# Feed-forward stage of a four-layer kernel: layer norm's moments of samples 3 to 8 made by matmuls with a constant tile, root by ScalarE

## The chip, the core and the metric

The kernel runs on one core of a Trainium2 chip. The metric is device time in microseconds (us) of one execution. Five engines work from queues of their own, each in order: TensorE (PE; its weight loads, PEld, overlap its matmuls), VectorE (DVE), ScalarE (ACT), GpSimd (POOL) and SyncE (SP), which issues the DMAs. They wait for one another through semaphores written out by hand.

## What is computed

Eight samples of 512 tokens by 512 channels pass through a rotation, a conditioned residual block, a low-rank steering layer and a transformer block. The change lies in the last layer's feed-forward part:

```python
def layernorm(x, gamma, beta):
    mu = jnp.mean(x, axis=-1, keepdims=True)
    var = jnp.var(x, axis=-1, keepdims=True)
    return (x - mu) * jax.lax.rsqrt(var + EPS) * gamma + beta
x1 = x + attn_out
h2 = layernorm(x1, gamma2, beta2)
ff = jax.nn.gelu(h2 @ W1 + b1, approximate=False) @ W2 + b2
x2 = x1 + ff
return x + g * (x2 - x)
```

All is float32. Products keep that accuracy by splitting each operand into a high part, rounded to the matmul's type (`F32R`), and the low rest, and taking three matmuls: high by high, high by low, low by high.

## The kernel before

A sample `x` of the feed-forward stage lies in SBUF with its channels over the 128 partitions: `x[:, j, :]` for j = 0 to 3 holds 128 channels by 512 tokens. Layer norm takes its moments over the channels, so over the partitions and over j.

In the code samples are b = 0 to 7. Samples b = 0 and 1 have paths of their own. From b = 1 on the first layer's product with W1 is made in 2x2 blocks by seven products in place of eight: a pair of hidden tiles is made by `product(pair, k)`, k in the order 1, 6, 7, 4, 5, 2, 3, each six matmuls of 256 columns. VectorE adds them up in five steps, `partial_of(pair, 0)` to `partial_of(pair, 4)`; steps 3 and 4 leave the two finished hidden tiles, one after the other. ScalarE takes Gelu of each and rounds it (`pair_high(pair, True)`, then `pair_high(pair, False)`: k_act, k_act_hi), VectorE makes the low rest (`pair_low`: k_act_lo), and TensorE multiplies with W2 (`second_product`, twelve matmuls of 512 columns for each hidden tile, cut into halves "0, 1" and "2, 3").

One sample is eight such pairs, called periods p = 0 to 7 here. `period(b, p)` writes out the order of each engine; n is the pair whose second product is running, n + 1 the one that is made meanwhile. TensorE in a period: product 1, product 6, second product of the first hidden tile (0, 1), product 7, (2, 3), product 4, product 5, second product of the second tile (0, 1), product 2, product 3, (2, 3). VectorE: `pair_low(n, False)`, `partial_of(n+1, 0)` and 1, then 2 and 3, `pair_low(n+1, True)`, `partial_of(n+1, 4)`. ScalarE: `pair_high(n, False)`, `copy_first(n+1)`, `pair_high(n+1, True)`. Products 4 and 5 write over the places in PSUM of products 1 and 6: product 4 waits until `partial_of(n+1, 0)` is done (L2237's first 256-column add of a pair). Product 1 waits for `partial_of(n, 3)`, product 7 for `partial_of(n, 4)`, product 2 for `partial_of(n+1, 1)`. The second product of a hidden tile waits for its `pair_low` (L2216).

Layer norm of the next sample is put between, in periods 2 to 5: `add_attention` (p = 2: x plus attention's result), `tokens` (TensorE turns x, sixteen 128x128 transposes, eight at the end of p = 2 and eight in p = 3, L2451), `statistics` (VectorE's mean and variance of each token from PSUM, two tiles at the start of p = 3 and two near its end, L2164 and L2166), the root by GpSimd (variance plus epsilon to the power -0.5, 128x4, L2100 and L2102), `spread` (p = 4: eight transposes that turn mean and root back and repeat them over the partitions, L2467 and L2471), `centre` (p = 4, after `partial_of(n+1, 3)`: x minus mean, four VectorE operations, L2177), `normalise` (p = 5, four more, L2183), ScalarE's `scale`, then the splitting into blocks.

`samples()` runs these periods for b = 2 to 7, which prepares samples b = 3 to 7 (five of them). The periods of b = 1 and before, which prepare b = 2, are written out one by one in `vector_tail`, `scalar_tail` and `tensor_tail`, mixed with the making of W1's factors for pairs 5 to 7 (`factor_high`, `factor_low`, `factor_sums`).

Of the kernel before, what the change touches and what calls it, by code (L numbers as in the profile page):

```python
# [18 lines left out]
P = 128  # L19
# [1906 lines left out]
def feed_forward_engines(nc, ctx, io, keep, psum, attention):  # L1926
# [29 lines left out]
    whole_tile = keep["stack_f"][1][:, 7, :]  # L1956
    partial = rows_of(keep["raw"][:, 2:4, :, :])[:, 6:8, :].rearrange("p n (h s) -> p (n h) s", h=2)
# [16 lines left out]
    added, summed, biased, gated = sem("added"), sem("summed"), sem("biased"), sem("gated")  # L1974
    given_ld, factor_sum, factor_hi, factor_lo = sem("given_ld"), sem("factor_sum"), sem("factor_hi"), sem("factor_lo")
# [30 lines left out]
    made_of = lambda part: given[part[1]][:, :, part[2], :].rearrange("p k a c -> p a k c")  # L2006

# [85 lines left out]
    def gpsimd(pool):  # L2093
        for b in range(B):
# [3 lines left out]
            if b + 1 < B:  # L2098
                pool.wait_ge(mv_set, T * (b + 1))
                pool.tensor_scalar(var[:], mv[:, :, 1], LN_EPS, None, ALU.add).then_inc(var_set, 1)  # L2100
                pool.wait_ge(var_set, b + 1)
                pool.tensor_tensor(rstd[:], var[:], keep["minus_half"][:], ALU.pow).then_inc(rstd_set, 1)  # L2102

    def vector(dve):
# [54 lines left out]
        def statistics(b, t):  # L2159
            if b == 1:  # L2160
                dve.wait_ge(tok_set, t + 1)
            else:
                dve.wait_ge(tin_full, T * (b - 1) + t + 1)
            dve.bn_stats(st[:, t, :], tok[:, t, :] if b == 1 else turn(t)).then_inc(stat_set, 1)  # L2164
            dve.wait_ge(stat_set, T * (b - 1) + t + 1)
            dve.bn_aggr(mv[:, t, :], st[:, t, :]).then_inc(mv_set, 1)  # L2166

# [6 lines left out]
        def centre(b):  # L2174
            dve.wait_ge(tback_full, J + 2 * (b - 2) + 1)
            for j in range(J):
                dve.tensor_tensor(tok[:, j, :], x[:, j, :], turn(0), ALU.subtract).then_inc(normed, 1)  # L2177

        def normalise(b):
            dve.wait_ge(tback_full, J + 2 * (b - 1))  # L2180
            for j in range(J):
                dve.wait_ge(normed, T + 2 * J * (b - 2) + j + 1)
                dve.tensor_tensor(tok[:, j, :], tok[:, j, :], turn(1), ALU.mult).then_inc(normed, 1)  # L2183
# [63 lines left out]
        def period(b, p):  # L2247
# [7 lines left out]
            if more and p == 3:  # L2255
                statistics(b + 1, 0)
                statistics(b + 1, 1)
# [15 lines left out]
            if more and p == 2:  # L2273
                add_attention(b + 1)
            if more and p == 5:
# [8 lines left out]
            if more and p == 3:  # L2284
                statistics(b + 1, 2)
                statistics(b + 1, 3)
# [21 lines left out]
        return steps(w1_low, w2_low, factor_low, factor_sums, add_attention, start_result, statistics, normalise_first, block_low, block_sums,  # L2308
                     split, finish, pair_low, partial_of, centre, normalise, samples)

    def scalar(act):
# [29 lines left out]
        def tokens(t):  # L2341
# [3 lines left out]
            act.activation(tok[:, t, :], turn(t), ACT.Copy).then_inc(tok_set, 1)  # L2345

# [56 lines left out]
        def period(b, p):  # L2403
# [4 lines left out]
            if n + 1 < HALF * (B - 1):  # L2408
                copy_first(n + 1)
            if n in EARLY_PARTS:  # L2410
# [22 lines left out]
        return steps(w1_high, w2_high, factor_high, tokens, scale, block_high, gelu, copy_first, pair_high, samples)  # L2433

    def tensor(pe):
        def tokens(b, t):
            if t == 0:
                pe.wait_ge(mid_set, J * b)
                if b == 1:
                    attention["results_taken"](pe)  # L2440
                elif b == 2:
                    pe.wait_ge(h_set, J)
                else:
                    pe.wait_ge(normed, T + 2 * J * (b - 2))
            if t >= 2:
                if b == 1:
                    pe.wait_ge(tok_set, t - 1)
                else:
                    pe.wait_ge(stat_set, T * (b - 1) + t - 1)
# [13 lines left out]
        def spread(b):  # L2463

            pe.wait_ge(mv_set, T * b)
            for t in range(T):
                last = pe.transpose(turn(0)[:, t * P:(t + 1) * P], mv[:, t, 0:1].to_broadcast([P, P]), ident[:])  # L2467
            last.then_inc(tback_full, 1)
            pe.wait_ge(rstd_set, b)
            for t in range(T):  # L2470
                last = pe.transpose(turn(1)[:, t * P:(t + 1) * P], rstd[:, t:t + 1].to_broadcast([P, P]), ident[:])  # L2471
            last.then_inc(tback_full, 1)
# [57 lines left out]
        def period(b, p):  # L2530
# [8 lines left out]
            second_product(at, m[0], 0, 1)  # L2539
            if first:  # L2540
# [15 lines left out]
            if more and p == 2:  # L2556
                tokens(b + 1, 0)
                tokens(b + 1, 1)
# [6 lines left out]
        return steps(tokens, back, spread, first_product, second_product, product, samples)  # L2565
# [570 lines left out]
def vector_tail(att, ff):  # L3136
# [83 lines left out]
    ff.statistics(1, 0)  # L3220
# [7 lines left out]
    for k in range(1, 4):  # L3228
        ff.statistics(1, k)
# [80 lines left out]
    ff.partial_of(3, 3)  # L3310
    ff.factor_low(6, 0)
    ff.pair_low(3, True)
    ff.partial_of(3, 4)
    ff.statistics(2, 0)
    ff.statistics(2, 1)
# [4 lines left out]
    ff.statistics(2, 2)  # L3320
# [3 lines left out]
    ff.statistics(2, 3)  # L3324
# [8 lines left out]
    ff.factor_low(7, 0)  # L3333
    ff.normalise(2)
    ff.partial_of(5, 4)
# [279 lines left out]
def scalar_tail(att, ff):  # L3615
# [164 lines left out]
    ff.pair_high(2, False)  # L3780
    ff.factor_high(6, 0)
# [782 lines left out]
```

## Time and profile before

| | |
|---|---|
| median of 3 runs | 1610.72 us (1610.68 to 1611.48) |
| span of the profiled execution | 1610.9 us |
| TensorE busy in it | 1585.8 us (98%) |
| VectorE, ScalarE, GpSimd busy | 1166.6, 982.8, 410.9 us |
| mean granted TensorE clock | 0.995 |
| feed-forward periods of samples | from about 1010 us to the end, one sample in about 86.5 us |

How to read it: times of the views count from the span's start. A matmul's own time holds the way through the array; the distance from one start to the next says what it takes of TensorE when the queue is full. The chain of waits gives such distances. VectorE's operations overlap by about 0.08 us where one does not need the other's result.

### The profile page before, as it was taken

To read this page: it belongs to the slowest core of one execution; us is meant where nothing else is said; L and a number is where in the kernel's file an instruction comes from. 1 tells how busy PE (TensorE), PEld (TensorE's weight loads), DVE (VectorE), ACT (ScalarE), POOL (GpSimd) and SP (SyncE) were. 2 spreads that over 40 slices of the span, in tenths; PEclk is the share of its full clock that TensorE was granted. 3 is DMA by queue.
4 is the path that set the end of the run, shared out by engine and by line. 5 is a ranking of instruction groups with operands and counts; after the bars stand their busy time and mean duration, and the time that the engine had idled before them with its cause. 6 is when DMAs were issued, how large, how long until landed. Compare 5 with 4: busy or idle time off the path is not lost.

```text
span 1610.9 us, 27177 instructions
## 1 busy us (share of the span) xinstructions
PE 1585.8 (98%) x9296; PEld 1299.5 (81%) x9298; DVE 1166.6 (72%) x2767; ACT 982.8 (61%) x2331; POOL 410.9 (26%) x605
## 2 busy tenths in 40 slices
PE   7999999999999999999999999999999999999999
PEld 4688786777777777777777688898999999999998
DVE  7999888786969686868778576785655656565643
ACT  6888766887878787878778755352433324242422
POOL 8998810313222313131312110201010110202010
PEclk8999999999999999999999999999999999999999
DMA  7042135543545444444337435866464555556361
GB/s 308 0 183 97 66 126 126 149 130 92 138 95 139 100 115 122 111 116 115 88 90 214 167 152 207 303 262 232 178 234 170 213 225 188 212 178 265 142 211 68
DMA packets 62257, 254.79 MB, mean 158 GB/s; under 512 B 10628, under 2 KB 16004, under 8 KB 46760
## 3 DMA queue, kind: packets, MB, share of 16 engines
q1 hardware_dynamic: 62120, 253.06, 48.2%
q8 instruction: 74, 1.21, 0.3%
q14 instruction: 63, 0.52, 0.1%
HBM read 153.93 MB, written 48.23 MB: 125 GB/s over the span
## 4 chain that ended last, share of the span: by engine, by line
PE 90%; POOL 3%; DMA 2%; DVE 2%; ACT 1%; issue 1%; SPq 1%; POOLq 0%; DVEq 0%; ACTq 0%
PE psum L83 24%; PE psum L84 23%; PE psum L85 23%; PE psum L1529 5%; PE psum L1549 5%; PE psum L1579 4%; PE psum L1470 1%; DMA k_weights<-w_factors 1%; PE psum L1478 1%; PE psum L2451 1%; DMA k_raw<-in_t_w 1%; POOL k_gs_square L252 1%; POOL k_gs_root L247 1%; ACT psum L1229 1%; POOL k_gs_scaled L256 1%
## 5 line engine op out<-in xcount | busy, mean ns | idle before, releaser
L1229 ACT ACTIVATE psum<-psum,b_mx 128x512 f32<-128x512 f32 (+3 forms) x512 | 258.9, 509 | 63.2 <-DVE b_mx L990 62.0
L990 DVE CUSTOM_DVE_ANT_0 psum<-psum,b_mask 128x512 f32<-128x512 f32 (+3 forms) x512 | 244.7, 506 | 53.0 <-PE psum L1529 48.1
L2398 ACT ACTIVATE k_act<-k_stack_f,k_smalls 128x512 f32<-128x512 f32 x112 | 80.9, 722 | 303.6 <-DVE k_stack_f L2237 297.1
L1241 ACT ACTIVATE k_exps<-psum 128x512 f32<-128x512 f32 (+1 forms) x384 | 194.6, 532 | 59.4 <-PE psum L1549 58.1
L864 POOL TENSOR_SCALAR_AFFINE_SELECT k_exps<-k_exps 128x256 f32<-128x256 f32 x256 | 96.4, 413 | 381.0 <-ACT k_exps L1241 379.1
L2097 POOL TENSOR_SCALAR k_result<-k_result,k_pb 128x512 f32<-128x512 f32 x32 | 59.2, 1866 | 434.9 <-DVE k_result L2156 434.9
L2216 DVE TENSOR_TENSOR k_act_lo<-k_act,k_act_hi 128x512 fp32r<-128x512 f32 x112 | 77.2, 690 | 120.6 <-ACT k_act_hi L2401 120.6
L83 PE MATMUL psum<-k_act_hi,k_w_hi 128*128 128x512 f32 x384 | 150.8, 393 | 0.0
L84 PE MATMUL psum<-k_act_lo,k_w_hi 128*128 128x512 f32 x384 | 150.5, 392 | 0.0
L85 PE MATMUL psum<-k_act_hi,k_w_lo 128*128 128x512 f32 x384 | 150.2, 391 | 0.0
L2237 DVE TENSOR_TENSOR k_raw<-psum,k_raw 128x256 f32<-128x256 f32 x168 | 70.5, 421 | 106.0 <-PE psum L85 95.4
L1529 PE MATMUL psum<-k_stack 96*128 96x512 f32 (+3 forms) x512 | 142.6, 330 | 3.1 <-DMA k_stack<-k_samples 2.0
L85 PE MATMUL psum<-k_normed,k_weights 128*128 128x512 f32 (+1 forms) x384 | 144.3, 376 | 0.0
L1549 PE MATMUL psum<-k_stack 98*128 98x512 f32 (+3 forms) x512 | 134.8, 332 | 0.6 <-ACT k_exps L1241 0.3
L83 PE MATMUL psum<-k_normed,k_weights 128*128 128x512 f32 (+1 forms) x320 | 126.0, 394 | 0.0
L84 PE MATMUL psum<-k_normed,k_weights 128*128 128x512 f32 (+1 forms) x320 | 120.0, 375 | 0.0
L1529 PEld LDWEIGHTS psum<-k_stack 96*128 96x128 f32 x512 | 93.6, 190 | 29.9 <-issue 8.8
L1549 PEld LDWEIGHTS psum<-k_stack 98*128 98x128 f32 x512 | 91.0, 189 | 27.7 <-issue 9.6
L1229 ACT ACTIVATION_READ_ACCUMULATOR psum<-psum,b_mx 128x1 f32 x512 | 108.6, 212 | 0.0
L85 PEld LDWEIGHTS psum<-k_act_hi,k_w_lo 128*128 128x128 f32 x384 | 72.1, 188 | 16.2
L85 PEld LDWEIGHTS psum<-k_normed,k_weights 128*128 128x128 f32 x384 | 73.0, 190 | 14.1
L83 PE MATMUL psum<-k_h,k_stack 128*128 128x256 f32 x294 | 82.6, 281 | 0.0
(372 smaller groups left out, 4418.2 us busy)
## 6 DMA issues: line engine op xcount, KB each, us to landing
k_stack<-w_factors SPq DMA_DIRECT2D x35, 1792.0 KB, 7.7
k_stack<-k_samples SPq DMA_DIRECT2D x384, 128.0 KB, 2.4
k_weights<-w_factors SPq DMA_DIRECT2D x17, 1792.0 KB, 7.5
x<-k_tokens SPq DMA_DIRECT2D x10, 1024.0 KB, 4.3
k_tokens<-x SPq DMA_DIRECT2D x8, 1024.0 KB, 5.1
d<-k_result SPq DMA_DIRECT2D x32, 256.0 KB, 2.9
k_raw<-x SPq DMA_DIRECT2D x8, 1024.0 KB, 4.8
k_raw<-d SPq DMA_DIRECT2D x8, 1024.0 KB, 7.1
```

Source lines behind the costliest of these rows:

```text
L83: pe.matmul(out, w_hi, x_hi, start=start and k == 0, stop=False)
L84: pe.matmul(out, w_hi, x_lo, start=False, stop=False)
L85: last = pe.matmul(out, w_lo, x_hi, start=False, stop=stop and k == n - 1)
L864: pool.affine_select(out=own, in_=own, compare_op=ALU.is_ge, fill=0.0, base=0, pattern=[[0, 2], [1, P]], channel_multiplier=-1).then_inc(c ...
L990: last = dve.tensor_tensor_reduce(got, got, mask[:, S - width:S], -INV_SQRT_DH, -2.0 * MASKED, ALU.add, ALU.min, mx[n % 2][:, h, t:t + 1])
L1229: act.activation(sc(n, u)[:, at:at + width], sc(n, u)[:, at:at + width], ACT.Exp, bias=mx[n % 2][:, h, t:t + 1], scale=-1.0, accum_out=sum ...
L1241: act.activation(exps[n % 2][:, h, at:at + width], by_key(n, u)[:, 0:width], ACT.Exp, scale=INV_SQRT_DH).then_inc(k_act, 1)
L1529: last = pe.matmul(sc(n, u)[:, at:at + width], stack[n % 2][0:3 * DH, 2 * h, t * P:(t + 1) * P], stack[n % 2][0:3 * DH, 2 * h + 1, 0:width ...
L1549: last = pe.matmul(by_key(n, u)[:, at:at + width], stack[n % 2][0:3 * DH + 2, 2 * h + 1, j * P:(j + 1) * P], stack[n % 2][0:3 * DH + 2, 2 ...
L2216: dve.tensor_tensor(act_lo[n % 2], act_f[:], act_hi[n % 2].bitcast(F32), ALU.subtract).then_inc(act_lo_set, 1)
L2237: dve.tensor_tensor(out, got, other, ALU.add).then_inc(partial_set, 1)
L2398: act.activation(act_f[:], whole_tile, ACT.Gelu, bias=small(smalls, "b1", 2 * pair % M + second)).then_inc(pair_gelu, 1)
```

## The change

For samples b = 2 to 7 layer norm's moments no longer pass through turned tokens. The sums over j are made by VectorE, the sum over the partitions by a matmul with a tile that holds 1/512 everywhere (`mean_of`), which leaves the mean repeated in every partition. ScalarE squares x, VectorE adds the squares, a second pair of matmuls gives the mean square. Root: ScalarE's Ln and Exp (-0.5 times) from one table set, named in the code, then one step of refinement by VectorE. The mean (x's sum) and the squares' sum are split in high and low, two matmuls of 512 columns each. Moved: `tokens`, `statistics` and `spread` are gone for these samples; `token_sum` stands in p = 2 after `partial_of(n+1, 3)`, `square_sum` at the start of p = 3, `variance` in p = 4 between `partial_of(n+1, 0)` and 1, `refine` in p = 4 ahead of `partial_of(n+1, 2)`. GpSimd has no part of it any more.

```diff
+        def token_sum(b):
+            dve.wait_ge(mid_set, J * (b - 1) + 2)
+            dve.tensor_tensor(sum_f, x[:, 0, :], x[:, 1, :], ALU.add).then_inc(sums_set, 1)
+            for j in (2, 3):
+                dve.wait_ge(mid_set, J * (b - 1) + j + 1)
+                wait_sums(dve, b, j - 1)
+                dve.tensor_tensor(sum_f, sum_f, x[:, j, :], ALU.add).then_inc(sums_set, 1)
+            wait_sums(dve, b, 3)
+            dve.tensor_copy(sum_hi, sum_f).then_inc(sums_set, 1)
+            wait_sums(dve, b, 4)
+            dve.tensor_tensor(sum_lo, sum_f, sum_hi.bitcast(F32), ALU.subtract).then_inc(sums_set, 1)
+        def square_sum(b):
...
+        def variance(b):
+            dve.wait_ge(tback_full, J + 2 * (b - 2) + 2)
+            wait_squares(dve, b, J)
+            dve.tensor_tensor(var_f, turn(1), sum_f, ALU.subtract).then_inc(stat_set, 1)
+            wait_statistics(dve, b, 1)
+            dve.tensor_scalar(var_f, var_f, 0.0, LN_EPS, ALU.max, ALU.add).then_inc(stat_set, 1)
+        def refine(b):
+            wait_rough(dve, b, 2)
+            dve.tensor_tensor(var_f, var_f, sum_f, ALU.mult).then_inc(stat_set, 1)
+            wait_statistics(dve, b, 3)
+            dve.scalar_tensor_tensor(var_f, var_f, -0.5, sum_f, ALU.mult, ALU.mult).then_inc(stat_set, 1)
+            wait_statistics(dve, b, 4)
+            dve.scalar_tensor_tensor(sum_f, var_f, 1.5, sum_f, ALU.add, ALU.mult).then_inc(stat_set, 1)
@@ vector, period
             if more and p == 3:
-                statistics(b + 1, 0)
-                statistics(b + 1, 1)
+                square_sum(b + 1)
...
+                if more and p == 4:
+                    variance(b + 1)
                 partial_of(n + 1, 1)
...
+            if more and p == 4:
+                refine(b + 1)
...
-            if more and p == 3:
-                statistics(b + 1, 2)
-                statistics(b + 1, 3)
+            if more and p == 2:
+                token_sum(b + 1)
             if more and p == 4:
                 centre(b + 1)
@@ scalar
+        def squares(b):
+            for j in range(J):
+                act.wait_ge(mid_set, J * (b - 1) + j + 1)
+                act.activation(tok[:, j, :], x[:, j, :], ACT.Square).then_inc(tok_set, 1)
+        def rough_rstd(b):
+            act.preload_act_table_set("natural_log_exp_and_others")
+            wait_statistics(act, b, 2)
+            act.activation(sum_f, var_f, ACT.Ln).then_inc(rstd_set, 1)
+            wait_rough(act, b, 1)
+            act.activation(sum_f, sum_f, ACT.Exp, scale=-0.5).then_inc(rstd_set, 1)
+            act.preload_act_table_set("gelu_and_others")
@@ tensor
+        def mean_product(b):
...
+            wait_sums(pe, b, 5)
+            pe.matmul(turn(0), mean_of[:], sum_hi, start=True, stop=False)
+            pe.matmul(turn(0), mean_of[:], sum_lo, start=False, stop=True).then_inc(tback_full, 1)
+        def square_product(b):
+            wait_sums(pe, b, 10)
+            pe.matmul(turn(1), mean_of[:], squares_r[:, 1, :], start=True, stop=False)
+            pe.matmul(turn(1), mean_of[:], squares_r[:, 2, :], start=False, stop=True).then_inc(tback_full, 1)
@@ tensor, period
+            if more and p == 4:
+                square_product(b + 1)
             if first:
                 product(n, 7)
             second_product(at, m[0], 2, 3)
             if more and p == 3:
-                tokens(b + 1, 2)
-                tokens(b + 1, 3)
-            if more and p == 4:
-                spread(b + 1)
+                mean_product(b + 1)
...
-            if more and p == 2:
-                tokens(b + 1, 0)
-                tokens(b + 1, 1)
```

`square_sum` has the five operations of `token_sum`, on the squares and in place. ScalarE's `squares` stand in p = 2 and one more `mean_square` (the mean's square, from PSUM) in p = 3, both between `copy_first` and `pair_high(n+1, True)`; `rough_rstd` is there in p = 4. The lists written out for b = 2 get the same steps: `token_sum(2)` after `partial_of(3, 3)`, `square_sum(2)` ahead of `partial_of(4, 0)`, `variance(2)` ahead of `pair_low(4, True)`, `refine(2)` after `factor_low(7, 0)`, and `partial_of(5, 4)` ahead of `normalise(2)` instead of behind it.

## Rows read from the trace of the kernel before

**Rows 1.** Page, part 1: busy time, share of the span and instructions of each engine.
```profile
PE 1585.8 (98%) x9296; PEld 1299.5 (81%) x9298; DVE 1166.6 (72%) x2767; ACT 982.8 (61%) x2331; POOL 410.9 (26%) x605
```
**Rows 2.** Busy time by stretch: PE, PEld, DVE, ACT, POOL, then clock, DMA.
```profile
1280.00:1370.00 90.00, 90.00 (x573) 81.31 (x572) 53.82 (x98) 32.11 (x53) 8.91 (x6) 1.00 0.58 214
```
**Rows 3.** Chain of waits, one sample: start, time it takes, what.
```profile
1300.19 0.23 PE psum L85
1300.43 0.87 PE psum L2451 x8
```
**Rows 4.** Timeline of PE, periods 3 to 5 of one sample: start, duration, operation.
```profile
1302.57 0.39 PE L83 MATMUL psum<-k_act_hi,k_w_hi 128*128 128x512 f32 x1
...
1306.83 0.36 PE L83 MATMUL psum<-k_weights 128*128 128x256 f32 x1
...
1315.37 0.28 PE L83 MATMUL psum<-k_normed,k_stack 128*128 128x256 f32 x1
...
1325.40 0.39 PE L83 MATMUL psum<-k_act_hi,k_w_hi 128*128 128x512 f32 x1
```
**Rows 5.** Timeline of DVE, periods 2 to 6 of the same sample; brackets: idle time before.
```profile
1297.03 0.68 DVE L2237 TENSOR_TENSOR k_stack_f<-psum,k_raw 128x512 f32<-128x512 f32 x1
1299.30 0.69 DVE L2216 TENSOR_TENSOR k_act_lo<-k_act,k_act_hi 128x512 fp32r<-128x512 f32 x1 [1.58 <-ACT k_act_hi L2401]
...
1302.17 0.69 DVE L2216 TENSOR_TENSOR k_act_lo<-k_act,k_act_hi 128x512 fp32r<-128x512 f32 x1 [1.59 <-ACT k_act_hi L2401]
...
1304.41 0.95 DVE L2237 TENSOR_TENSOR k_raw<-psum,k_raw 128x256 f32<-128x256 f32 x2
...
1319.95 0.42 DVE L2237 TENSOR_TENSOR k_raw<-psum,k_raw 128x256 f32<-128x256 f32 x1 [3.17 <-PE psum L85]
...
1323.27 0.68 DVE L2216 TENSOR_TENSOR k_act_lo<-k_act,k_act_hi 128x512 fp32r<-128x512 f32 x1
...
1339.36 0.69 DVE L2197 TENSOR_TENSOR k_tokens<-k_tokens 128x512 f32<-128x512 f32 x1
1340.09 0.69 DVE L2199 TENSOR_TENSOR k_tokens<-k_tokens 128x512 f32<-128x512 f32 x1
```
**Rows 6.** Single lines of the code: count, duration in ns (shortest/median/longest), first and last start.
```profile
L907 DVE CAST b_steer<-k_row_f x1: 424/424/424, 40.7 to 40.7; 2x512 fp32r<-2x512 f32 x1
L2171 DVE TENSOR_SCALAR k_tokens<-k_tokens,b_mv,b_rstd x4: 544/546/549, 952.0 to 953.4; 128x512 f32<-128x512 f32 x4
L2156 DVE SCALAR_TENSOR_TENSOR k_result<-k_raw,k_pb x32: 742/747/1100, 924.3 to 1545.2; 128x512 f32<-128x512 f32 x32
L2371 ACT ACTIVATE k_h<-k_tokens x28: 613/616/636, 974.3 to 1514.7; 128x512 fp32r<-128x512 f32 x28
L2380 ACT ACT_TABLE_LOAD  x1: 1283/1283/1283, 905.8 to 905.8; - x1
```
**Rows 7.** Timeline of DVE, the written-out part that prepares sample b = 2.
```profile
1042.47 0.69 DVE L2164 BATCH_NORM_STATS2 b_st<-psum 128x6 f32<-128x512 f32 x1
...
1044.09 0.40 DVE L2237 TENSOR_TENSOR k_raw<-psum,k_raw 128x256 f32<-128x256 f32 x1
...
1063.30 0.42 DVE L2237 TENSOR_TENSOR k_raw<-psum,k_raw 128x256 f32<-128x256 f32 x1 [0.37 <-ACT k_raw L2391]
```
**Rows 8.** Timeline of PE and ACT in the same part.
```profile
1044.55 0.39 PE L83 MATMUL psum<-k_h,k_weights 128*128 128x256 f32 x1
1064.70 0.28 PE L83 MATMUL psum<-k_h,k_stack 128*128 128x256 f32 x1
1039.46 0.42 ACT L2335 ACTIVATE k_stack<-b_mask 128x256 fp32r<-128x256 f32 x1 [7.43 <-DMA k_early<-in_w]
```
**Rows 9.** Early stage: PE's longest wait, and the two stretches from there (columns as in 2).
```profile
10.33 1.87 PE L541 MATMUL psum<-k_sines,k_raw 128*128 128x8 f32 x8 [3.69 <-DMA k_raw<-in_t_w]
...
10.00:20.00 10.00, 7.22 (x25) 3.49 (x27) 8.38 (x21) 9.13 (x15) 8.60 (x10) 0.50 1.01 422
20.00:30.00 10.00, 9.77 (x68) 6.01 (x69) 7.92 (x16) 6.33 (x10) 8.41 (x11) 0.99 1.02 421
```

More of the change, by code:

```diff
@@ new lines, in square_sum @@
+        def square_sum(b):
+            wait_squares(dve, b, 1)
+            dve.tensor_tensor(tok[:, 0, :], tok[:, 0, :], tok[:, 1, :], ALU.add).then_inc(sums_set, 1)
+            for j in (2, 3):
+                wait_squares(dve, b, j)
+                wait_sums(dve, b, 4 + j)
+                dve.tensor_tensor(tok[:, 0, :], tok[:, 0, :], tok[:, j, :], ALU.add).then_inc(sums_set, 1)
+            wait_sums(dve, b, 8)
+            dve.tensor_copy(squares_r[:, 1, :], tok[:, 0, :]).then_inc(sums_set, 1)
+            wait_sums(dve, b, 9)
+            dve.tensor_tensor(squares_r[:, 2, :], tok[:, 0, :], squares_r[:, 1, :].bitcast(F32), ALU.subtract).then_inc(sums_set, 1)
@@ L2306, in samples @@
                 finish(B - 1, j)
-        return steps(w1_low, w2_low, factor_low, factor_sums, add_attention, start_result, statistics, normalise_first, block_low, block_sums,
+        return steps(w1_low, w2_low, factor_low, factor_sums, add_attention, start_result, statistics, token_sum, square_sum, variance, refine, normalise_first, block_low, block_sums,
                      split, finish, pair_low, partial_of, centre, normalise, samples)
@@ L2409, in period @@
                 copy_first(n + 1)
+            if more and p == 2:
+                squares(b + 1)
+            if more and p == 3:
+                mean_square(b + 1)
+            if more and p == 4:
+                rough_rstd(b + 1)
             if n in EARLY_PARTS:
@@ L2539, in period @@
             second_product(at, m[0], 0, 1)
+            if more and p == 4:
+                square_product(b + 1)
             if first:
@@ L2563, in samples @@
                     period(b, p)
-        return steps(tokens, back, spread, first_product, second_product, product, samples)
+        return steps(tokens, back, mean_product, square_product, first_product, second_product, product, samples)
     return {"sync": sync, "gpsimd": gpsimd, "vector": vector, "scalar": scalar, "tensor": tensor}
@@ L3219, in vector_tail @@
     ff.w1_low(4)
-    ff.statistics(1, 0)
+    ff.statistics(0)
     ff.split(4)
@@ L3228, in vector_tail @@
     for k in range(1, 4):
-        ff.statistics(1, k)
+        ff.statistics(k)
     ff.split(6)
@@ L3310, in vector_tail @@
     ff.partial_of(3, 3)
+    ff.token_sum(2)
     ff.factor_low(6, 0)
@@ L3313, in vector_tail @@
     ff.partial_of(3, 4)
-    ff.statistics(2, 0)
-    ff.statistics(2, 1)
+    ff.square_sum(2)
     ff.partial_of(4, 0)
@@ L3323, in vector_tail @@
         ff.partial_of(4, k)
-    ff.statistics(2, 3)
+    ff.variance(2)
     ff.pair_low(4, True)
@@ L3333, in vector_tail @@
     ff.factor_low(7, 0)
+    ff.refine(2)
+    ff.partial_of(5, 4)
     ff.normalise(2)
-    ff.partial_of(5, 4)
     ff.factor_low(7, 1)
@@ L3780, in scalar_tail @@
     ff.pair_high(2, False)
+    ff.squares(2)
     ff.factor_high(6, 0)
@@ L3786, in scalar_tail @@
     ff.factor_high(6, 2)
+    ff.mean_square(2)
     ff.pair_high(4, True)
@@ L3790, in scalar_tail @@
     ff.pair_high(4, False)
+    ff.rough_rstd(2)
     ff.factor_high(7, 0)
     ff.factor_high(7, 1)
+    ff.pair_high(5, True)
     ff.scale(2, 0)
-    ff.pair_high(5, True)
     ff.scale(2, 1)
@@ L4383, in tensor_tail @@
     ff.second_product(22, 7, 2, 3)
-    ff.tokens(2, 2)
+    ff.mean_product(2)
     ff.product(4, 5)
```

89 lines of the change are left out of this document (44 added, 45 removed).

## Prediction

> **What bounds the kernel now.** I read the page's busy shares first: TensorE 98%, VectorE 72%, ScalarE 61% [rows 1]. Then busy time by stretch in the part that the change touches: of 90 us TensorE is busy 90.00, VectorE 53.82, ScalarE 32.11 [rows 2]. So here TensorE alone sets the end: a microsecond taken from its queue is a microsecond of the kernel, provided it never waits. Third, the chain of waits: it runs through TensorE's matmuls and through the transposes, which take 0.87 us for eight [rows 3]. Last the timelines of the engines through one sample [rows 4, 5], because the change gives work to an engine on which TensorE depends, and an average share does not say whether that work falls at a moment with room.
>
> **TensorE's side, which gains.** Removed for each of six samples: 24 transposes, three times 0.87, together 2.61 us. Added: four matmuls of 512 columns at 0.23 each [rows 3], 0.92 us. Net 1.69 us a sample, 10.1 us in all, if nothing waits. For the five samples of the loop, place by place: TensorE is 0.87 early from period 3 on, 0.87 - 0.46 more after `mean_product` in the middle of period 3, and 0.87 - 0.46 more after period 4.
>
> **VectorE's side: the sizes.** A chain of dependent 512-column adds starts every 0.73 us (1339.36, 1340.09 [rows 5]); so three adds 2.18. The copy that rounds: the only row of a cast from SBUF to fp32r of this length takes 0.42, on two partitions [rows 6]; I take it with 0.04 for the dependence, 0.46, and 0.73 as upper end, that of an add; below 0.42 there is no row of a 512-element operation. The subtraction holds the queue for 0.61 more (0.69 less the 0.08 of overlap). Sum of `token_sum`, and of `square_sum`: 3.25 us each, 3.52 by the upper end. The Trainium skill, page "VectorE: DVE Perf Modes", section "Mode 2×_2P — use both read ports for one tensor", says that an operation with one source, all in SBUF, makes two results in a cycle in fp32 too, and that one with two tensors cannot. By it the cast stays at the row's length on 128 partitions and the sums at 3.25; without it they would be 3.52 and each stall below 0.5 longer. No row here shows the cast on 128 partitions. `variance`: 0.73 and 0.55 [rows 6]. `refine`: 0.73 + 0.79 + 0.67 = 2.2, with 0.75 for the two three-operand steps [rows 6]. Removed: `statistics`, four times 0.8. VectorE has room for the sum in 86 us; what counts is the place.
>
> **Period 2, `token_sum`.** Before, `partial_of(n+1, 3)` starts at 1297.03 and VectorE then sits 1.58 us until `pair_low(n+1, True)` at 1299.30 [rows 5]. Now VectorE is free at 1297.03 + 0.60 = 1297.63, works until 1300.88, and `pair_low` starts there: 1.58 late, done at 1301.57. TensorE wants it at 1302.57 [rows 4] less 0.87 = 1301.70. It just fits; no stall, but the slack is used up. ScalarE's four squares (0.62 each, as its rounding copies [rows 6]) follow the adds of `add_attention` one by one and end before Gelu's input is there: nothing. The second hidden tile's chain (`partial_of(n+1, 4)`, Gelu, rounding) starts 1.58 later too, so `pair_low(n, False)` of period 3 starts at 1302.17 + 1.58 = 1303.75 [rows 5].
>
> **Period 3, `square_sum`: the step that decides.** It stands ahead of `partial_of(n+1, 0)`, and product 4 may not start before that is done. VectorE is through with `pair_low` at 1304.36, with the squares at 1307.61; `partial_of(n+1, 0)` ends at 1308.03, and with 0.1 for the signal (it took 0.06 from 1044.09 + 0.40 to 1044.55 [rows 7, 8]) product 4 can start at 1308.1. Before it was done by 1304.41 + 0.42 = 1304.83 [rows 5], two microseconds ahead of product 4 at 1306.83 [rows 4]. Now TensorE arrives there at 1306.83 - 0.87 - 0.87 + 0.46 = 1305.55. It stalls for 2.55 us and goes on 1.3 us later than before. Everything that VectorE and ScalarE do next hangs on products 5 to 3, so it moves by the same 1.3.
>
> **Period 4, `variance`, root, `refine`.** The square product stands after the second product's first half, before ended at 1315.37 [rows 4]: now 1315.37 + 1.3 + 0.46 = 1317.1. `variance` runs from 1317.3 to 1318.6. `partial_of(n+1, 0)` is already through and 1 is not urgent. Ln and Exp at 0.65 each (bounds 0.62 and the 0.72 of a Gelu with a bias) end at 1320.05. `refine` holds VectorE until 1322.25, where before `partial_of(n+1, 2)` came at 1319.95 [rows 5]: 2.3 us late, and with it `partial_of(n+1, 3)`, Gelu, `centre`. `pair_low(n+1, True)` starts at 1323.27 + 2.3 = 1325.57 and is there at 1326.36; TensorE, which is now 1.3 - 0.41 = 0.89 later than before, wants it at 1325.40 + 0.89 = 1326.29 [rows 4, 5]. Stall 0.1; up to 0.7 with the longer lengths. The two table loads (1.28 us each [rows 6]) cost nothing: the first lies ahead of Ln while ScalarE would wait for `variance` anyway, the second between Exp at 1320.05 and Gelu's input near 1323.3. If that cover were gone, each would add its 1.3 us to the same chain. `centre` and `normalise` keep their lengths; for periods 6 and 7 I take no stall and have no rows for it here; 0.4 us a sample go into the upper end.
>
> Sum for one sample of the loop: 2.55 + 0.1 - 1.69 = +0.96, near 1.0; five of them +5.0. GpSimd's two small operations go, and are priced at nothing: they lay beside TensorE's work.
>
> **The written-out part (b = 2).** `token_sum` fits: ScalarE and VectorE wait for a DMA until 1039.46 there, after 7.43 us of idle ScalarE [rows 8], and TensorE's first groups of transposes only shorten the way to that same date, so part of the 1.69 is not gained. `square_sum` takes the place of two statistics that held VectorE from 1042.47 to 1044.09 [rows 7]: 3.25 for 1.62, so `partial_of(4, 0)` and product 4, which restarted at 1044.55 right behind it [rows 8], are 1.65 late. Fewer transposes behind it (sixteen gone at 1.74, two pairs of matmuls come at 0.92) bring that to +0.8. Then `variance` (1.2) ahead of `pair_low(4, True)` and `refine` (2.2) ahead of `normalise(2)`, less the other two statistics, push `partial_of(6, 0)` from 1063.30 [rows 7] to about 1066.8; product 4 of pair 6 stood at 1064.70 [rows 8] + 0.8 = 1065.5 and can start at 1067.3: a stall of 1.8. Sum +2.6; the factors' DMA of pair 7, which moves with `factor_low(6, 3)` by 2 us, can add to it: 2 to 4, I take 2.7.
>
> **Forecast.** +5.0 + 2.7 = +7.7 us on the span of 1610.9, which is the median of the runs (1610.7) within 0.2: 1618.4 us, slower by 0.5%. Its own range: the loop's samples +0.6 (a stall shorter by 0.4) to +2.0 (the cast as long as an add makes 0.5 more in period 3, period 5 and the unworked periods add another 0.5 together), the written-out part 2 to 4: 1615.9 to 1624.9.
>
> **Rivals.** (a) The cover holds, the change gives what it takes from TensorE: 10.1 us, 1600.6. It needs `partial_of(n+1, 0)` of period 3 to be done 2.5 us sooner than I place it. For it: VectorE is idle 40% of the time [rows 2]. Against: queues are in order and product 4's wait is in the code. Chance 0.09. (b) Stall and saving cancel: the sums take 0.6 each in place of 0.73 for dependent adds, both sums 1 us shorter together, and period 3's stall is about 1.5: 1609 to 1613. Against: dependent adds of this length show 0.73 [rows 5]. Chance 0.08. (c) Slower by more, through the clock. After TensorE's wait of 3.69 us the stretch from 10 to 20 us shows 0.50, which is 1.2 GHz in place of 2.4, and 0.99 again in the stretch after [rows 9]. If a stall of 2.5 us did the same, each of the seven would cost up to half of ten microseconds: about +30, 1640 or more. Against: the wait in the early stage is half as long again, and the ones before us would each stand alone between stretches of full work. The Trainium skill, page "TensorE: Matmul & The Clock Gate", states such a gate with these two levels, and the trace agrees on the levels. Chance 0.04. (d) The change doesn't do what it says, that is, a step is late because the compiler adds table loads or the square is not in Gelu's set: one load more in period 2, 1.3 us more before Gelu there, and then `pair_low(n+1, True)` is late by up to 1.3 in period 3; the later stall takes that up in part: 1620 to 1625, inside the forecast's range. Chance 0.05, the forecast itself 0.74.
>
> **How the numbers follow.** Slower by over 0.2% (3.2 us; about what a measurement of this kernel can tell from no change) are the forecast, (c) and (d): 0.83. Same 0.08, faster 0.09. The range: the forecast's own with (d) holds 0.79 less what its bounds leave out; I reach down into (b), to 1612, and to 1625 at the top.
>
> **What would show it.** In the profile after: TensorE waits some 2.5 us for VectorE's 256-column add (L2237's line) once in each sample, at a product's first matmul; `token_sum` and `square_sum` of 3.2 us each on VectorE, the latter right ahead of that add; a stretch of 90 us with TensorE busy about 87; clock 1.00; table loads of 1.28 with no TensorE wait behind them. Wrong if TensorE's busy stretches stay at 90.00 of 90 (then a), if the stall in period 3 is about 1.5 (b), or if the clock falls (c); wrong in its second term if period 5 shows a stall of a microsecond.

## The result, and the profile after

| | before | after |
|---|---|---|
| median | 1610.7 us (4 runs, 1609.9 to 1611.5) | 1626.6 us (4 runs, 1625.6 to 1628.6) |
| span of the profiled execution | 1610.9 us | 1623.9 us |
| mean granted TensorE clock | 0.995 | 0.991 |
| ratio of the times | | 1.010 [1.009, 1.011] |

Slower by 1.0%, twice the 0.5% that was forecast, and 1.6 us above the end of the range. A second round of the changed kernel (below) gave 1626.2. The profiled spans differ by 13.0 us and the medians by 15.9, because the execution profiled after had reached the feed-forward samples early: its first result of sample b = 0 is written at 1005.2 us against 1008.3 before. In the profiled executions of all the kernels below that date lies between 1003.4 and 1008.3 us, though none of them changes that first part. So all that follows is counted from there on: before 602.64 us are left, after 618.67, that is +16.0.

The page's first line of the kernel after (as [rows 1]):

```profile
PE 1583.6 (98%) x9178; PEld 1294.7 (80%) x9178; DVE 1203.3 (74%) x2809; ACT 1021.9 (63%) x2385; POOL 400.9 (25%) x594
```

TensorE's share is the same 98% as before; nothing of a 16 us loss can be read from it. The same 90 us as in [rows 2], the next ones below it short stretches (PE, PEld, DVE, ACT, POOL, then clock, DMA):

```profile
1280.00:1370.00 90.00, 87.70 (x540) 78.85 (x539) 58.62 (x102) 37.92 (x60) 7.24 (x4) 0.98 0.54 201
...
1306.00:1311.00 5.00, 5.00 (x32) 4.45 (x32) 3.38 (x6) 1.63 (x3) 0.00 (x0) 1.00 0.91 347
1314.40:1317.90 3.50, 3.50 (x15) 3.36 (x16) 0.94 (x3) 0.00 (x0) 0.00 (x0) 0.52 0.00 0
1318.00:1323.00 5.00, 5.00 (x35) 4.56 (x34) 1.82 (x4) 2.72 (x4) 0.00 (x0) 1.00 0.32 86
```

TensorE was busy 90.00 of 90 us and is busy 87.70: the missing 2.30 us are the forecast stall. The new thing is the third row: "busy" 3.50 of 3.50, at a granted clock of 0.52, that is 1.2 GHz in place of 2.4, right behind the stall. Busy time hides it.

All waits of TensorE from 900 us on (engine, tile, line waited for: us in total, times, longest):

```profile
PE psum L83 <- DVE k_raw L2297: 14.9, 7, 2.4
PE psum L83 <- DMA k_weights<-w_factors: 1.6, 1, 1.6
PE psum L83 <- DVE k_act_lo L2276: 0.7, 1, 0.7
```

There are seven waits for VectorE's 256-column adds (L2297 here, L2237 of before): five in the loop, as forecast, and two in the written-out part. TensorE's timeline at one of them (as [rows 4], start, duration, operation; brackets: idle time before):

```profile
1311.42 0.39 PE L2546 MATMUL psum<-k_weights,c_mean_of 128*128 128x512 f32 x1
1311.65 0.40 PE L2547 MATMUL psum<-k_stack,c_mean_of 128*128 128x512 f32 x1
1314.35 0.58 PE L83 MATMUL psum<-k_weights 128*128 128x256 f32 x1 [2.30 <-DVE k_raw L2297]
1314.73 0.41 PE L84 MATMUL psum<-k_weights 128*128 128x256 f32 x1
1314.94 0.41 PE L85 MATMUL psum<-k_weights 128*128 128x256 f32 x1
...
1317.07 0.63 PE L83 MATMUL psum<-k_act_hi,k_w_hi 128*128 128x512 f32 x1
1317.50 0.53 PE L84 MATMUL psum<-k_act_lo,k_w_hi 128*128 128x512 f32 x1
1317.87 0.39 PE L85 MATMUL psum<-k_act_hi,k_w_lo 128*128 128x512 f32 x1
...
1318.80 0.28 PE L83 MATMUL psum<-k_weights 128*128 128x256 f32 x1
1318.92 0.28 PE L84 MATMUL psum<-k_weights 128*128 128x256 f32 x1
```

Two losses stand in it. The first is the wait: the last mean product should hand over at 1311.65 + 0.23 = 1311.88 and the next matmul starts at 1314.35, 2.47 us later (the row's 2.30 counts from the modelled end of the matmul; so each wait costs 0.17 more than its row says). The second is the pace after it: 256-column matmuls start every 0.21 us (1314.73, 1314.94) where they start every 0.12 at 1318.80. From 1314.35 to 1317.07 twelve of them take 2.72 us in place of 1.40, the next two, of 512 columns, 0.80 in place of 0.46: together 1.65 us.

VectorE in periods 2 and 3 of the same sample (as [rows 5]):

```profile
1303.63 0.68 DVE L2189 TENSOR_TENSOR k_stack_f<-k_raw 128x512 f32<-128x512 f32 x1
1304.42 1.49 DVE L2193 TENSOR_TENSOR k_stack_f<-k_stack_f,k_raw 128x512 f32<-128x512 f32 x2
1305.94 0.43 DVE L2195 CAST k_weights<-k_stack_f 128x512 fp32r<-128x512 f32 x1
1306.40 0.69 DVE L2197 TENSOR_TENSOR k_stack<-k_stack_f,k_weights 128x512 fp32r<-128x512 f32 x1
1307.01 0.68 DVE L2276 TENSOR_TENSOR k_act_lo<-k_act,k_act_hi 128x512 fp32r<-128x512 f32 x1
...
1310.49 0.69 DVE L2201 TENSOR_TENSOR k_tokens<-k_tokens 128x512 f32<-128x512 f32 x1
1311.28 1.49 DVE L2205 TENSOR_TENSOR k_tokens<-k_tokens 128x512 f32<-128x512 f32 x2
1312.81 0.43 DVE L2207 CAST k_tokens_r<-k_tokens 128x512 fp32r<-128x512 f32 x1
1313.27 0.69 DVE L2209 TENSOR_TENSOR k_tokens_r<-k_tokens,k_tokens_r 128x512 fp32r<-128x512 f32 x1
1313.88 0.88 DVE L2297 TENSOR_TENSOR k_raw<-psum,k_raw 128x256 f32<-128x256 f32 x2
```

`square_sum` holds the queue from 1310.49 to 1313.88, and `partial_of(n+1, 0)`, the add at 1313.88, releases TensorE at 1314.35.

From sample to sample, counted between the first results written of two samples; the second row is the written-out part, the third the five samples of the loop:

| | before | after |
|---|---|---|
| b = 0 to 1 | 86.95 | 91.60 (+4.65) |
| five samples, together | 433.28 | 444.65 (+11.37, 2.27 each) |
| TensorE's waits in those five, by their rows | none | 2.13, 2.25, 2.30, 2.24, 0.68, 2.38 |
| of these followed by 1.2 GHz | | four (not 0.68 and 2.38) |

(The last sample takes 76.8 us in both.) The sum closes to 0.2 us: the loop's six waits are 11.98 by their rows and 1.0 by the 0.17 each; TensorE's relief takes off five times 1.69, 8.45; that leaves 4.5 of 11.4, and four stretches at 1.2 GHz at 1.65 are 6.6 more.

### The profile page after: what moved, and what is told of

It is laid out like the page before. It is cut to its first block, busy times and chain, and to the rows that moved or that the text cites. A ratio compares the mean times of both kernels' runs of the same rounds, so it can differ in the third digit from the quotient of the medians.

```text
span 1623.9 us, 27054 instructions
## 1 busy us (share of the span) xinstructions
PE 1583.6 (98%) x9178; PEld 1294.7 (80%) x9178; DVE 1203.3 (74%) x2809; ACT 1021.9 (63%) x2385; POOL 400.9 (25%) x594
## 4 chain that ended last, share of the span: by engine, by line
PE 82%; DVE 7%; POOL 3%; DMA 3%; issue 2%; ACT 2%; SPq 1%; DVEq 0%; POOLq 0%; ACTq 0%
PE psum L83 22%; PE psum L84 21%; PE psum L85 21%; PE psum L1529 5%; PE psum L1549 5%; PE psum L1579 4%; DMA k_raw<-d 1%; PE psum L1470 1%; PE psum L1478 1%; DVE k_raw L2166 1%; DMA k_raw<-in_t_w 1%; POOL k_gs_square L252 1%; DMA k_stack<-k_samples 1%; POOL k_gs_root L247 1%; SPq L779 1%
## 5 line engine op out<-in xcount | busy, mean ns | idle before, releaser
L2297 DVE TENSOR_TENSOR k_raw<-psum,k_raw 128x256 f32<-128x256 f32 x168 | 70.5, 421 | 72.4 <-PE psum L85 61.2
L85 PEld LDWEIGHTS psum<-k_act_hi,k_w_lo 128*128 128x128 f32 x384 | 72.8, 189 | 16.5
```

Source lines behind the costliest of these rows:

```text
L85: last = pe.matmul(out, w_lo, x_hi, start=False, stop=stop and k == n - 1)
L2297: dve.tensor_tensor(out, got, other, ALU.add).then_inc(partial_set, 1)
```

## The experiments

Three questions: is the place of `square_sum` the whole cause, do the table loads cost anything, and is the clock the missing part of the sum? All of them are kernels of their own beside runs of before on the same chip. "Loop" is the time of the five samples together, as in the table above, against 433.28 before.

### The squares' sum behind the urgent adds

```diff
-            if more and p == 3:
-                square_sum(b + 1)
 ...
                 partial_of(n + 1, 1)
+            if more and p == 3:
+                square_sum(b + 1)
```

> The changed kernel with one edit in the loop: square_sum of period 3 stands after the second 256-column add of the pair (partial_of(n+1, 1)) instead of ahead of the first. The arithmetic is the same. Theory (the place of square_sum makes TensorE wait 2.3 us in each of five samples, and the clock that falls behind the wait costs 1.7 more in most): both go from the five samples, the written-out part keeps its two waits of 1.8; with 8.4 us of removed transposes and matmuls in the loop the time is 1603 to 1607 us, the clock 1.00 in the loop. Rival 1 (VectorE has too much work in periods 2 to 5 wherever it stands: 7 us more a sample): the wait comes back at the second product of period 4 or 5, 1 us or more a sample, time 1610 or more. Rival 2 (TensorE's clock fell for another reason than the wait): the waits go and the 1.2 GHz stretches stay, 1610 to 1613.

Measured: 1606.9 us (before beside it 1611.2), ratio 0.997 [0.996, 0.999]; loop 426.42, -6.9. TensorE's waits in the whole feed-forward part, and its 90 us:

```profile
PE psum L83 <- DVE k_raw L2297: 3.5, 2, 1.8
PE psum L83 <- DMA k_weights<-w_factors: 2.2, 1, 2.2
PE psum L83 <- DVE k_act_lo L2276: 0.6, 1, 0.6
...
1280.00:1370.00 90.00, 89.89 (x562) 80.81 (x561) 62.00 (x109) 37.83 (x60) 9.80 (x5) 1.00 0.56 210
```

The five waits of the loop are gone, and no stretch of it is at 1.2 GHz; the two of the written-out part, which this kernel leaves alone, stay. The same work in another place of the same queue is worth 18.2 us in five samples (444.65 to 426.42), of which some 12 were stall; the rest, near four times 1.6, went with it. The median is inside what was expected and both rivals are out.

### The written-out part too

The loop as above; in the written-out part `square_sum(2)` goes behind `partial_of(4, 1)`, `normalise(2)` behind `pair_low(5, True)`, and ScalarE's `copy_first(6)` ahead of its `scale(2, 0)`.

```diff
-    ff.square_sum(2)
     ff.partial_of(4, 0)
 ...
     ff.partial_of(4, 1)
+    ff.square_sum(2)
 ...
-    ff.normalise(2)
     ff.factor_low(7, 1)
     ff.partial_of(6, 0)
     ff.pair_low(5, True)
+    ff.normalise(2)
```

> As the run with the squares later, and the same for the part written out for b = 2: square_sum(2) after partial_of(4, 1), normalise(2) after factor_low(7, 1), partial_of(6, 0) and pair_low(5, True), and ScalarE's copy_first(6) ahead of scale(2, 0). Theory: the two waits of 1.8 us go, 3 to 3.6 us less than that run, 1600 to 1602.5, that is 9 to 10 us under the kernel before: all that TensorE was relieved of. Rival: the DMA of W1's factors (a wait of 1.58 us at 1035 us, 0.5 before) sets the date there, and half of it comes back as a longer wait for a DMA or for the factors of pair 7: 1603 to 1604.

Measured: 1604.9 us, ratio 0.996 [0.995, 0.998]; b = 0 to 1 takes 87.83 (91.60 in the changed kernel, 86.95 before), loop 426.47. The two waits of 1.8 are gone, smaller ones of 1.21 and 0.62 stand in their place, and the part still costs 0.9 more than before. The time is above both what was expected (at most 1602.5) and its rival (1603 to 1604), and the rival's cause isn't the one: the wait for the factors' DMA at 1035 us is 0.35 here. Both places together make the changed kernel 6 us faster than the kernel before.

### Without the tables

The loop as in the first experiment, and the root left out: two squares stand in place of Ln and Exp, with no table load around them, so this kernel doesn't compute layer norm.

```diff
-            act.preload_act_table_set("natural_log_exp_and_others")
 ...
-            act.activation(sum_f, var_f, ACT.Ln).then_inc(rstd_set, 1)
+            act.activation(sum_f, var_f, ACT.Square).then_inc(rstd_set, 1)
 ...
-            act.activation(sum_f, sum_f, ACT.Exp, scale=-0.5).then_inc(rstd_set, 1)
-            act.preload_act_table_set("gelu_and_others")
+            act.activation(sum_f, sum_f, ACT.Square, scale=-0.5).then_inc(rstd_set, 1)
```

> As the run with the squares later, but the root's Ln and Exp are two Squares of the same size, and the two table loads of each sample are left out (left out of the computation: the root; the values are not layer norm's). Theory (both table loads, 1.28 us each, lie in ScalarE's idle time): within 0.5 us of that run. Rival: a switch of tables costs more than its 1.28 us row, or Gelu of period 4 waits for the second load: 5 to 6 us less (five samples by 1.1 to 1.3).

Measured: 1605.4 us, ratio 0.996 [0.995, 0.998]; loop 426.20 against 426.42 with the tables. In the loop ten table loads are worth 0.2 us together, which is nothing. (The median is 1.5 us below the first experiment's, more than the 0.5 expected. In the two profiled executions the difference lies ahead of the change: the first result is written at 1003.4 against 1005.6 us, and what follows takes 600.0 against 599.5.) ScalarE's timeline in the changed kernel shows why (start, duration; brackets: idle time before):

```profile
1323.72 1.28 ACT L2419 ACT_TABLE_LOAD   x1
1326.30 0.63 ACT L2421 ACTIVATE k_stack_f<-k_raw 128x512 f32<-128x512 f32 x1 [1.30 <-DVE k_raw L2217]
1326.96 0.63 ACT L2423 ACTIVATE k_stack_f<-k_stack_f 128x512 f32<-128x512 f32 x1
1327.62 1.28 ACT L2424 ACT_TABLE_LOAD   x1
1330.80 0.72 ACT L2477 ACTIVATE k_act<-k_stack_f,k_smalls 128x512 f32<-128x512 f32 x1 [1.90 <-DVE k_stack_f L2297]
```

Behind the first load ScalarE is still idle for 1.30 us until `variance` is done (L2217, at 1326.27), behind the second for 1.90 until Gelu's input is there: both lie in time that it would have waited anyway.

### Only the delay: adds put into the kernel before

To price the stall without anything else of the change, dependent 512-column adds, whose results nobody uses, go into the kernel before at the place of `square_sum`, four, six or eight a sample (0.73 us each).

```diff
                 statistics(b + 1, 0)
                 statistics(b + 1, 1)
+                for i in range(4):
+                    dve.tensor_tensor(tok[:, 0, :], x[:, 0, :], x[:, 1, :], ALU.add).then_inc(dose, 1)
+                    dve.wait_ge(dose, 4 * (b - 2) + i + 1)
```

Four:

> The kernel before with four dependent 512-column adds of VectorE (0.73 us each, 2.9 in all, their result is not used) put ahead of the first 256-column add in period 3 of five samples; nothing else is changed. VectorE had 1.9 us of room there, so TensorE should wait 1.0 us in each. Theory (the wait costs its length, and behind a wait of over about 2 us the clock falls to 1.2 GHz for a stretch): clock stays at 1.00, time +4 to +6 us. Rival (any wait of TensorE at this place costs more than its length): +8 or more.

Six:

> The same with six adds, 4.4 us: a wait of 2.4 us in each of five samples, as long as in the changed kernel, without any of its other edits. Theory: waits 12 us, and after most of them a stretch of about 3.5 us at 1.2 GHz, half of it lost, 1.7 each: +17 to +21 us. Rival (the lower clock comes from the change's other work, not from the wait): +12, clock 1.00.

Eight:

> The same with eight adds, 5.8 us: a wait of 3.9 us in each. Theory: waits 19.5 us, a lower clock behind every one of them, again near 1.7 each or somewhat more: +26 to +31 us. Rival (the clock's loss grows with the length of the wait): over +35. Rival without the clock: +19.5.

| adds | median us (before beside it 1611.5) | runs | ratio | waits of the loop, by their rows | loop | 1.2 GHz behind |
|---|---|---|---|---|---|---|
| 4 | 1614.8 | 8 | 1.002 [1.000, 1.003] | 0.26, 0.36, 0.26, 1.09, 0.26 | +3.6 | none |
| 6 | 1623.5 | 4 | 1.008 [1.006, 1.010] | 1.94, 1.83, 1.72, 2.00, 1.72 | +10.6 | none |
| 8 | 1634.0 | 2 | 1.013 [1.009, 1.017] | 3.34, 3.29, 3.17, 3.53, 3.17 | +24.1 | four of five |

Waits and 90 us with six adds, then with eight (here L2238 is the line of the 256-column adds):

```profile
PE psum L83 <- DVE k_raw L2238: 9.2, 5, 2.0
...
1280.00:1370.00 90.00, 88.28 (x562) 79.56 (x561) 56.95 (x102) 31.86 (x52) 8.91 (x6) 1.00 0.55 203
```

```profile
PE psum L83 <- DVE k_raw L2238: 16.5, 5, 3.5
...
1280.00:1370.00 90.00, 86.83 (x542) 78.11 (x541) 57.13 (x102) 31.29 (x51) 8.91 (x6) 0.98 0.51 191
...
1315.90:1320.00 4.10, 4.10 (x17) 3.67 (x18) 2.17 (x6) 0.72 (x1) 0.00 (x0) 0.60 0.02 4
```

With six adds the waits explain the loss to 0.5 us: 9.2 + 5 x 0.17 = 10.1 of 10.6, and the clock stays at 1.00. With eight, 16.5 + 0.9 = 17.4 of 24.1; 6.7 is left over four stretches at 1.2 GHz, 1.7 each. The waits came out shorter than expected (1.0, 2.4 and 3.9 us), all but one, and all three times below what was expected. With six adds it is the rival's outcome that came, +12.0 by the medians at a clock of 1.00: by itself that run would speak for the change's other work as the cause of the lower clock. But its waits were 1.7 to 2.0 us and not the 2.4 that were meant, and its profiled execution (1620.4) is the shortest of four, up to 1625.8. The run with eight decides: the kernel before has no layer norm by matrix products, and with waits of 3.2 to 3.5 us it shows the same stretches. So the lower clock needs none of the change's matmuls. A wait of 2.1 to 2.4 us in the kernel before was not made.

### A wait 0.7 us shorter in the changed kernel

The last operation of `square_sum`, the subtraction, goes behind `partial_of(n+1, 0)` in the loop; all else is the changed kernel.

```diff
             dve.tensor_copy(squares_r[:, 1, :], tok[:, 0, :]).then_inc(sums_set, 1)
+
+        def square_low(b):
             wait_sums(dve, b, 9)
 ...
+                if more and p == 3:
+                    square_low(b + 1)
```

> The changed kernel, but of square_sum's five operations only the last (the subtraction, 0.6 us of VectorE's queue) stands behind the first 256-column add of period 3, in the five samples of the loop. TensorE's wait should fall from 2.1 to 2.4 to about 1.6 us. Theory (a wait of over about 2 us is followed by a stretch at 1.2 GHz that costs some 1.7 us, a shorter one is not): 5 x 0.6 from the waits and 4 to 5 x 1.7 from the clock, 9 to 11 us less than the changed kernel run beside it; clock 1.00 in the loop. Rival (the clock falls behind any wait of this order, or for another cause): 3 us less, the stretches at 1.2 GHz stay.

Measured: 1617.7 us (before beside it 1611.3), ratio 1.003 [1.002, 1.005]; loop 435.33, 9.3 less than the changed kernel. Its TensorE at the same place, and the stretch behind the wait, then two stretches behind waits of 1.89 and 1.83 us in the written-out part:

```profile
1309.99 0.40 PE L2551 MATMUL psum<-k_stack,c_mean_of 128*128 128x512 f32 x1
1312.03 0.38 PE L83 MATMUL psum<-k_weights 128*128 128x256 f32 x1 [1.64 <-DVE k_raw L2299]
1312.25 0.28 PE L84 MATMUL psum<-k_weights 128*128 128x256 f32 x1
1312.37 0.28 PE L85 MATMUL psum<-k_weights 128*128 128x256 f32 x1
```

```profile
1312.10:1315.50 3.40, 3.40 (x23) 3.14 (x24) 1.83 (x4) 0.62 (x1) 0.00 (x0) 1.00 0.00 0
1044.50:1048.00 3.50, 3.50 (x12) 3.02 (x13) 3.16 (x7) 0.63 (x1) 0.00 (x0) 0.54 1.02 438
1067.30:1071.00 3.70, 3.70 (x17) 3.28 (x18) 3.01 (x7) 2.85 (x6) 0.00 (x0) 0.69 0.25 105
```

This run ties the lower clock to the length of the wait. The loop's five waits of 2.13 to 2.38 became 1.40 to 1.64, none is followed by 1.2 GHz, and 3.5 us less of waiting (11.98 to 8.45) gave 9.3 us. The other 5.8 are what four stretches at the lower clock had cost, to within 1 us of 4 x 1.65. Against the changed kernel measured beside it (last experiment) the medians differ by 8.5 us, a little less than the 9 to 11 expected, and the loops by 8.0: 3.5 of waiting and 4.5 for the three stretches that it had there.

### All sums at their best places

The second experiment, with `token_sum` of the loop one step later (behind `partial_of(n+1, 4)` of p = 2) and `square_sum(2)` behind `pair_low(3, False)`. It is meant for the wait of 0.6 to 0.8 us for `pair_low`'s k_act_lo that every version with `token_sum` in its first place has once, in the last sample.

```diff
-            if more and p == 2:
-                token_sum(b + 1)
 ...
                 pair_low(n + 1, True)
                 partial_of(n + 1, 4)
+            if more and p == 2:
+                token_sum(b + 1)
```

> All of the change's arithmetic, its steps placed where VectorE has room: in the loop token_sum behind partial_of(n+1, 4) of period 2 and square_sum behind partial_of(n+1, 1) of period 3; in the part for b = 2 square_sum behind pair_low(3, False), normalise behind pair_low(5, True), copy_first(6) ahead of the scales. Theory (only the places cost time): no TensorE wait in the loop, five samples at 1.6 to 1.7 us less than before each, the part for b = 2 within 1 us of before: 7.5 to 10 us under the kernel before, ratio 0.994 to 0.9955. Rival (token_sum in the new place delays pair_low(n, False) of period 3 or the mean's product, and a wait comes there): ratio 0.9965 or more, as the version with both places mended.

Measured: 1605.3 us, ratio 0.997 [0.995, 0.998]; loop 426.07, b = 0 to 1 87.42. The one wait in the loop shrank from 0.81 in the second experiment to 0.36, and TensorE's 90 us are full again:

```profile
1280.00:1370.00 90.00, 90.00 (x565) 81.09 (x564) 62.08 (x108) 38.51 (x61) 11.21 (x6) 1.00 0.56 207
```

It can't be told from the second experiment's 1604.9, and it is short of the 7.5 to 10 us under the kernel before that were expected: 5.9. Of the 8.45 us that TensorE was to be relieved of in the loop 7.2 arrive. The distances between the starts of TensorE's matmuls, added up over the loop of both kernels, say where the rest is: 0.5 is the one wait left, 0.2 the twenty new matmuls (4.8 for 4.6), and 0.5 the 960 other matmuls of 512 columns (221.6 against 221.1); the transposes gave back what was taken for them.

### The changed kernel once more

> The changed kernel itself once more, beside the two others on the same chip. Theory: 13 to 17 us over the kernel before, ratio 1.0085 to 1.0105, three to five of the five loop waits followed by 1.2 GHz. Rival (the number of falls of the clock differs much from run to run): a spread of its times of over 5 us.

Measured: 1626.2 us, ratio 1.009 [1.007, 1.012]. Waits of the loop 2.12, 2.24, 2.35, 2.24, 0.64, 2.37, the same as the first time within 0.05; but 1.2 GHz followed three of them (2.12, 2.24, 2.24) and neither 2.35 nor 2.37. Loop 443.29 against 444.65, 1.4 less for one stretch fewer. The four executions spread over 6.0 us, which was the rival's sign, and the slowest has the lowest mean clock (1630.8 at 0.988); but those of the kernel before beside it spread over 6.7 us, so the spread alone says little.

## Why the prediction was wrong, and where it was right, step by step

**TensorE's relief, -1.69 a sample: right but for 0.1.** With one wait of 0.36 left the loop is 1.44 a sample shorter; that wait takes 0.10 of the difference, and slightly longer distances between the starts of matmuls the rest (the experiment with all sums at their best places).

**Sizes on VectorE: nearly right.** `token_sum` took 1307.01 - 1303.63 = 3.38 us and `square_sum` 3.39, for 3.25. The rounding copy is as taken (1305.94 to 1306.40, 0.46; its row says 0.43, on 128 partitions now). The Trainium skill, page "VectorE: DVE Perf Modes", section "Mode 2×_2P — use both read ports for one tensor", gives an operation with one source in SBUF two results in a cycle, and one with two tensors not; the trace agrees, with 0.43 for the copy and 0.69 for the subtraction of the same size. The adds start every 0.79 and 0.76 where 0.73 was taken from other dependent adds. `refine` was shorter (1327.63 to 1329.69, 2.06 for 2.2).

**Period 2, no stall: right but for one sample.** In the last sample of the loop the second product of the first hidden tile waits 0.68 us for k_act_lo: the slack that the prediction called used up.

**Period 3, the stall of 2.55: right.** 2.47 in the sample shown, 2.30 to 2.55 in the five, at the matmul, for the add and because of the operation that the prediction named (the first experiment moves it, and the wait is gone).

**Period 5, a stall of 0.1, at most 0.7: none was seen.** Table loads, priced at nothing: nothing (the third experiment). The Trainium skill, page "ScalarE: Activation LUTs", section "What ACT_TABLE_LOAD costs", counts 2.66 us for each, of which 1.28 is the load and the rest a drain; the trace agrees on 1.28 and shows no drain that anything waited for.

**The written-out part, +2.7: it measured +4.65.** Its two stalls are the ones forecast (1.78 and 1.84 for 1.65 and 1.8). The wait for the factors' DMA grew from 0.50 to 1.58, since TensorE now gets there earlier and the transfer doesn't: that relief was not gained, as the prediction said for this place, with a total that came out 0.4 too low. And behind the first stall the clock fell, for 3.4 us (1044.73 to 1048.14), 1.6 more; without that the part is +3.1.

**The step that failed: the clock was kept out of the sum.** It stood there as rival (c), with a chance of 0.04 and a price of up to 5 us a stall, and neither the forecast nor its upper end of 1625 held any of it. In fact five of the seven stalls were followed by a stretch at 1.2 GHz, and each cost about 1.6 us. The five together are 4 x 1.65 + 1.6 = 8.2 us. Taken from the 16.0 measured from the first result on they leave +7.8, and the forecast was +7.7. So the sum was right in its mechanism and lacked one term. That it comes so close is in part luck. In the loop (11.37 - 4 x 1.65) / 5 = +0.95 is left a sample, for a forecast of +0.96, but small misses cancel in it: the stall of period 3 was 0.12 shorter than forecast and the 0.1 of period 5 did not come, while the one wait of period 2, forecast as none, adds 0.17 a sample and the relief fell short by 0.1.

Why it was mispriced: the only row of before with a fall that was read was the early stage's [rows 9], a wait of 3.69 and a stretch of ten microseconds at 0.50. The price was taken from that stretch, and the chance from the argument that 2.5 us is shorter than 3.69 and stands alone between full work. That argument had no row behind it: the feed-forward part of before has no wait above 0.50, so its clock of 1.00 tells nothing of a stall of 2.5. The same trace of before holds two more falls, outside the feed-forward part, which the prediction did not look for. The first, a matmul and then a stretch:

```profile
257.68 0.50 PE L1460 MATMUL psum<-b_p,b_steer 98*128 98x512 f32 x1 [1.40 <-DVE k_samples L1035]
...
259.00:262.50 3.50, 3.48 (x9) 2.91 (x10) 3.44 (x12) 1.76 (x5) 0.00 (x0) 0.52 0.86 188
```

The second is at 812.1 us, also 3.4 us long, 2.6 us behind a wait of 1.13. They show a wait shorter than 2.5 us with a fall behind it, and a stretch of 3.4 us, half of which, 1.7, is the most that one fall can cost, in place of 5. An unknown of this kind should have been bounded from both sides like the others, from nothing to a few microseconds for each of seven stalls; the range would then have reached past 1630.

The other rivals fell. (a), the cover holds: it needed `square_sum` not to stand ahead of the add, and the first experiment shows that this was what was in the way in the loop. But even with all sums at their best places 5.9 us come of its 10.1: the loop gives 7.2 of 8.45, and the written-out part costs 0.5 where it was to give 1.7. (b), shorter sums: they are longer. (d), more table loads: there are two a sample.

## What to carry to other kernels

A microsecond taken from the engine that bounds is lost where another engine's in-order queue delays what frees its buffers: put new work behind the operation that the bounding engine waits for, not ahead of it; here moving one call in the loop turned +16 us into -4, and a few more moves made -6 of it. When a forecast has stalls of TensorE in it, give the clock a term of its own for each, and look for its lower level in short stretches right behind the waits, since busy time and a mean clock of 0.991 don't show it. If the work has to stay where it is, splitting it so that the wait gets shorter can give back more than the wait.

## What the runs showed of the hardware that was not expected

Waits of TensorE of about two microseconds, alone between tens of microseconds of full work, can be followed by 3.4 us at 1.2 GHz. Counted by the distances of the matmuls' starts, each of the sixteen falls in the feed-forward part of these runs cost 1.5 to 1.7 us. There, over all profiled executions: of fourteen waits from 1.1 to 1.75 us none was followed by a fall; of twelve from 1.77 to 2.04 five were (1.78, 1.80, 1.83, 1.84 and 1.89, while 1.94 and 2.04 were not); of the ten from 2.12 to 2.38 in the changed kernel seven, and one of 2.16 for a DMA in the first experiment was not; of five above 3.1 us four. These lengths are no threshold for other parts: near 260 us six of the eleven executions show a fall behind a wait of 1.4 us, near 812 us three behind one of 1.1. The same program gave both outcomes for the same wait (in one execution 2.24 twice with, 2.35 and 2.37 without), so what decides is more than the length of the wait, and these runs don't settle it. The fall does not always come at once: behind a wait of 2.13 us the first matmuls go at full pace, and only then

```profile
1136.56 0.28 PE L84 MATMUL psum<-k_weights,k_stack 128*128 128x256 f32 x1
1136.68 0.28 PE L85 MATMUL psum<-k_weights,k_stack 128*128 128x256 f32 x1
1136.80 0.34 PE L83 MATMUL psum<-k_weights,k_stack 128*128 128x256 f32 x1
1136.94 0.41 PE L84 MATMUL psum<-k_weights,k_stack 128*128 128x256 f32 x1
1137.15 0.41 PE L85 MATMUL psum<-k_weights,k_stack 128*128 128x256 f32 x1
```

the distance grows from 0.12 to 0.21. The Trainium skill, page "TensorE: Matmul & The Clock Gate", section "A second HAM failure mode: psum-queue depth-cycling", tells of frequent short idle times between groups of matmuls that make the clock go back and forth between its two levels. The trace agrees on the two levels, but here the level changed behind single idle times of 1.8 to 2.4 us.
